# A second column of each gather chunk fetched row by row, shared by two queues

## The chip, the cores and the metric

The kernel runs on one core of one Trainium2 chip. The metric is the device time of one execution in microseconds (us). Before the change it is 22680.64 us, the median of three runs (22672.05, 22680.64, 22682.27).

## What is computed

Five graph layers run one after the other over the same graph of 12500 nodes (64 features each) and 412500 directed edges, sorted by destination. Four of them gather, for every edge, one row of a table by the edge's source node, weigh it, and sum over the edges of each destination:

```python
# RGAT, run twice (8 relations, 4 heads)
alpha = leaky_relu(qn[etype, dst] + kn[etype, src])
ex = exp(alpha - segment_max(alpha, dst)[dst]); attn = ex / segment_sum(ex, dst)[dst]
agg = segment_sum(attn[:, :, None] * xw[etype, src], dst)
# GAT, one head, no relations: the same with h[src]
# RGCN: segment_sum(xw[etypes, src] * norm, dst)
# GINE: segment_sum over src of relu(x[dst] + edge_feats), then a small two-layer network
```

Each layer's output is added to `x` after a layer norm and a relu at its input. The change touches the gathers of the first four layers.

## The kernel before

**Tiling.** The edges are padded to 128 partitions with 3224 edges each. A partition's edges are cut into 52 chunks (`CH`) of 62 columns (`J`), so a chunk is 128 x 62 edges. The layers are called CONV1, CONV2 (the two RGAT convolutions), GAT, RGCN and GINE. For each of the first four, a table is written to DRAM with one row per node, or per node and relation: 68 numbers (272 bytes) in CONV1 and CONV2, 65 (260 bytes) in GAT, 64 (256 bytes) in RGCN.

**A layer's chunk loop.** The loop body holds two chunks, b = 0 and b = 1, with their own half of the buffer `G` (part of the tile `region`), and runs 26 times.

- GpSimd (line 652, called from the loop at lines 764 to 773) waits on `idx_ready` for the chunk's indices and issues one indirect DMA per column, for columns 0 to 60 (`JP = J - 1` = 61 of them). Each brings 128 rows, one for each partition.
- SyncE (lines 605 to 619) fetches the last column, number 61, by 128 transfers of one row each. For each chunk it asks for a list of 128 row numbers from DRAM (607), waits for `idx_ready` (609) and for the list (611), and then eight times (`RUN` = 16) loads 16 row numbers into registers (613), copies them (614) and issues 16 row transfers (615). The source address is computed from the row number, times the length of a row, ahead of each transfer.
- In CONV1 alone, SyncE also issues one transfer per chunk (619) that writes zeros to a 2 MB stretch of `h_edge`, a table that GINE uses later.
- VectorE waits for all of the chunk's rows (semaphores `gathered` and `rows_in`), computes scores, weights and running sums, and releases the half of `G` by writing the indices of the chunk after next into `idx` (1911, in RGCN 1858), which raises `idx_ready`.
- ScalarE, in the layers with scores, copies last chunk's sums (870, 872) and sends them to DRAM (879), turns the query rows (896), asks for the next (899), spreads a mask (900), and then waits for VectorE's scores before it takes exponentials (905 to 908; 903 in GAT). In RGCN it copies matrices between the two steps of a ranking that TensorE and VectorE do in 16 quads of columns for the next chunk (944), and turns the four pieces of the sums (933, 936).

The order on each queue is the order of the code. A chunk can be consumed when both GpSimd's 61 columns and SyncE's 128 rows have landed. GpSimd and SyncE can each be up to two chunks ahead of VectorE, and no more.

The rows of all four layers' loops:

```python
for p0 in range(0, P, RUN):
    sp.load(indices, row_list[0:1, b, p0:p0 + RUN])
    for k, row in enumerate([sp.snap(r) for r in indices]):
        sp.dma_start(G[p0 + k:p0 + k + 1, b, J, :],
                     tables[l][bass.ds(row, 1), :]).then_inc(rows_in[l][b][2 * p0 // P], 16)
```

Of the kernel before, what the change touches and what calls it, by code (L numbers as in the profile page):

```python
# [9 lines left out]
BF16 = mybir.dt.bfloat16  # L10
ACT = mybir.ActivationFunctionType
# [53 lines left out]
JP = J - 1  # L65
RUN = 16
# [48 lines left out]
def build(nc, a, out):  # L115
    ctx = ExitStack()
    with ctx:
# [25 lines left out]
        row_lists = dram("row_lists", (2 * CH, P), I32)  # L143
# [23 lines left out]
        row_list = sb("row_list", [CH, 2, P], I32)  # L167
# [157 lines left out]
        act_s = sem("act_steps")  # L325
# [8 lines left out]
        rows_in = {l: [[sem(f"rows_in{l}_{b}_{k}") for k in range(2)] for b in range(2)] for l in SUMMED}  # L334
# [168 lines left out]

        block = ctx.enter_context(nc.Block())
# [3 lines left out]
        def _(sp):  # L508
# [13 lines left out]
            sp.dma_start(row_list[:, 1, :], a["src"].rearrange("(p c j) -> c p j", p=P, c=CH)[:, :, J - 1]).then_inc(loaded, 16)  # L522
            sp.dma_start(row_list[:, 0, :],
                         a["edge_type_8"].rearrange("(p c j) -> c p j", p=P, c=CH)[:, :, J - 1]).then_inc(loaded, 16)
# [6 lines left out]
            sp.dma_start(row_lists[0:CH, :], row_list[:, 0, :]).then_inc(list_in, 16)  # L531
            sp.dma_start(row_lists[CH:2 * CH, :], row_list[:, 1, :]).then_inc(list_in, 16)
            for l in LAYERS:
# [66 lines left out]
                kind = 0 if REL_OF[l] > 1 else CH  # L600
                for q in range(GP):
                    sp.wait_ge(stored[q], 16 * TURNS * (l + 1))
                if l == CONV1:
                    sp.wait_ge(list_in, 32)
                with sp.Fori(0, CH // 2) as i:
                    for b in range(2):
                        sp.dma_start(row_list[0:1, b, :], row_lists[bass.ds(i * 2 + (kind + b), 1), :]).then_inc(list_in, 16)
                        sp.wait_ge(idx_ready, i * 2 + ((CH + 2) * l + b + 1))
                        sp.sem_inc(chunk_begun, 1)
                        sp.wait_ge(list_in, i * 32 + 16 * (CH * l + b + 3))  # L610
# [39 lines left out]
        def _(pool):  # L650
# [55 lines left out]
            for l in LAYERS:  # L706
# [12 lines left out]
                if l == GINE:  # L719

                    pool.wait_ge(big_zero, 16 * CH)
# [56 lines left out]
        def _(act):  # L778
            steps = Steps(act, act_s)
# [29 lines left out]
            for l in LAYERS:  # L809
# [66 lines left out]

                def send_sums(i, b, O):
                    act.wait_ge(sum_ready, i * 2 + (CH * l + b + 1))
                    act.dma_start(sum_rows[:, bass.ds(i * (2 * J) + b * J, J), :], O).then_inc(sum_out, 16)

                if h:
# [9 lines left out]
                    act.wait_ge(loop_ok, l + 1)  # L891
                    def score_chunk(i, b, more):
                        nth = CH * l + b + 1
                        at = i * (2 * J) + b * J
                        act.wait_ge(e_in, i * 32 + 16 * nth)
# [4 lines left out]
                        act.copy(REP[:, 0:k, 1:J1], bc(cont[:, bass.ds(at, J)], 1, k)).then_inc(q_in, 1)  # L900
                        act.wait_ge(ex_in, i * 2 + nth)
# [16 lines left out]
                if l == RGCN:  # L918
# [27 lines left out]
                    def finish_chunk(i, b, ranks):  # L946
                        for n in range(NQ):
# [5 lines left out]
                        send_sums(i, b, O)  # L953

                    for n in range(NQ):
                        copy_turned(0, 0, n)
# [305 lines left out]
        def _(dve):  # L1262
# [37 lines left out]
            for g in range(TURNS):  # L1300
# [28 lines left out]
            stt(out=row_list[:, 0, :], in0=row_list[:, 1, :], scalar=float(REL), in1=row_list[:, 0, :], op0=ALU.mult,  # L1329
                op1=ALU.add).then_inc(lists_ready, 1)  # L1330
# [336 lines left out]
            for l in LAYERS:  # L1667
# [52 lines left out]
                nth = l  # L1720
                if l == RGCN:
                    dve.sem_inc(ew_free, 1)
# [113 lines left out]
                def weighted_sums(i, b, at, ranks):  # L1836
# [8 lines left out]
                    def piece_step(m):  # L1845
                        q = m // 2
                        if m % 2 == 0:
                            if q == 0:
                                dve.wait_ge(gathered[l][b], i * (16 * JP) + 16 * JP)
                                for half in range(2):  # L1850
                                    dve.wait_ge(rows_in[l][b][half], i * (8 * P) + 8 * P)
# [41 lines left out]
                with s.loop(CH // 2, 2 * per) as i:  # L1893
                    for b in range(2):
# [18 lines left out]
                        if h:  # L1913
# [33 lines left out]
                            for half in range(2):  # L1947
                                dve.wait_ge(rows_in[l][b][half], i * (8 * P) + 8 * P)
# [94 lines left out]
```

## Time and profile before

| | us |
|---|---|
| median of three runs | 22680.64 |
| span of the profiled execution | 22678.7 |
| GpSimd (POOL) busy | 16413.3 |
| VectorE (DVE) busy | 10606.0 |
| ScalarE (ACT) busy | 5421.1 |
| TensorE (PE) busy | 5315.0 |

The profile gives the span of its execution and no separate total; the span is 1.9 us below the median of the runs. The gather loops of CONV1, CONV2, GAT and RGCN run on GpSimd from 447 to 4411 us, 4779 to 8739, 9048 to 13008 and 13248 to 17208 us. GINE and the end fill the rest. "SPq" and "ACTq" are the instruction queues of SyncE and ScalarE; an instruction that issues a DMA is listed there and is not counted as busy time. A line of the timeline with x128 is merged from 128 instructions, and its second number is the time from the start of the first to the end of the last.

### The profile page before, as it was taken

The numbers are of one execution on the slowest core, as the hardware profiler recorded it, in microseconds if no ns is written. First come the engines' busy times: TensorE is split into PE (matmuls) and PEld (weight loads), VectorE is DVE, ScalarE is ACT, GpSimd is POOL, SyncE is SP. The second block draws the span as 40 slices with busy tenths as digits, with TensorE's granted clock in tenths as the row PEclk, the third lists the DMA queues.
The fourth block names the chain that finished last, engine by engine and source line by source line (L and its number), as shares of the span: only waits on it lengthen the run. The fifth ranks groups of instructions, "written<-read, shape, count | busy, mean of one in ns | idle before, by whom it ended". The sixth has DMA issues, their size and how long they took to land.

```text
span 22678.7 us, 201879 instructions
## 1 busy us (share of the span) xinstructions
PE 5315.0 (23%) x30665; PEld 3876.7 (17%) x30665; DVE 10606.0 (47%) x9480; ACT 5421.1 (24%) x4707; POOL 16413.3 (72%) x17069
## 2 busy tenths in 40 slices
PE   2000000020000001222222266666662222222201
PEld 1000000010000001222222255555552000000001
DVE  2444444324444443556566668888884111111167
ACT  1222222222222222111111132222221211121175
POOL 7777777677777776777777767777776777777733
PEclk9999999999999999666666655555555666666655
DMA  6333333332222222222222232222222222222164
GB/s 203 95 98 101 95 98 98 88 97 76 70 75 70 72 73 46 54 54 58 54 57 55 52 87 56 52 56 52 56 52 61 84 76 76 76 80 80 66 235 162
DMA packets 782414, 1839.84 MB, mean 81 GB/s; under 512 B 380834, under 2 KB 415306, under 8 KB 720302
## 3 DMA queue, kind: packets, MB, share of 16 engines
q0 software_dynamic: 544128, 569.36, 13.8%
q10 hardware_dynamic: 88736, 721.35, 8.1%
q1 hardware_dynamic: 148622, 541.43, 6.7%
q14 instruction: 915, 7.50, 0.1%
q8 instruction: 13, 0.21, 0.0%
HBM read 1007.43 MB, written 929.12 MB: 85 GB/s over the span
## 4 chain that ended last, share of the span: by engine, by line
POOL 55%; issue 24%; SPq 12%; DMA 3%; DVE 2%; PE 2%; ACT 1%; POOLq 0%; DVEq 0%; ACTq 0%
POOL region L652 41%; POOL by_src L742 12%; SPq L615 9%; SPq L613 3%; DMA region<-by_src 2%; DMA row_list<-row_lists 1%; POOL q_rel L713 1%; SPq L614 1%; PE ps L1207 1%; DVE region L1567 1%; DVE region L1538 0%; PE ps L1168 0%; POOL h_edge L725 0%; PE ps L1209 0%; POOL q_one L713 0%
## 5 line engine op out<-in xcount | busy, mean ns | idle before, releaser
L652 POOL DMA_INDIRECT region<-table,idx x12688 | 11972.1, 944 | 3941.9 <-issue 3873.2
L742 POOL DMA_INDIRECT by_src<-region,idx x3224 | 3122.7, 969 | 1007.9 <-issue 1001.5
L1950 DVE TENSOR_TENSOR region<-ps,region 128x248 f32<-128x248 f32 (+1 forms) x156 | 74.4, 477 | 3958.0 <-DMA region<-table,idx 1967.5
L1216 PE MATMUL ps<-ident,region 128*68 128x128 f32 (+1 forms) x3 | 1.3, 444 | 8044.9 <-DVE region L2013 8044.9
L1767 DVE TENSOR_TENSOR region<-ps,region 128x2048 bf16<-128x2048 f32 x833 | 1845.8, 2216 | 18.2 <-DVE region L1761 8.0
L870 ACT COPY region<-region 128x4216 f32<-128x4216 f32 (+1 forms) x156 | 1182.2, 7579 | 2477.7 <-DVE region L1996 2477.7
L1112 PE MATMUL ps<-region 98*128 98x128 f32 x6448 | 1657.9, 438 | 323.3 <-DVEq L1833 192.8
L1533 DVE CAST region<-src 128x62 f32 (+1 forms) x52 | 11.7, 224 | 3463.8 <-DMA by_src<-region,idx 3463.6
L1207 PE MATMUL ps<-region,ident 128*128 128x512 f32 (+1 forms) x832 | 809.5, 1062 | 3141.2 <-DVE region L1538 3141.2
L1112 PEld LDWEIGHTS ps<-region 98*128 98x128 f32 x6448 | 1455.9, 330 | 410.7 <-DVEq L1833 269.7
L1905 DVE TENSOR_TENSOR_SCAN region<-region,ps 128x1008 f32<-128x1008 f32 x624 | 1382.9, 2244 | 10.7
L1216 PEld LDWEIGHTS ps<-ident,region 128*68 128x68 f32 (+1 forms) x3 | 0.4, 150 | 8045.6 <-DVE region L2013 8045.6
L1902 DVE TENSOR_TENSOR ps<-region,ps 128x1008 f32<-128x1008 f32 x624 | 1192.1, 1940 | 105.2 <-ACT ps L906 96.2
L1916 DVE TENSOR_TENSOR_SCAN region<-region,ps 128x2016 f32<-128x2016 f32 x104 | 452.8, 4354 | 1582.6 <-ACT region L900 1582.6
L905 ACT ACTIVATE region<-ps 128x248 f32<-128x248 f32 (+1 forms) x156 | 50.5, 324 | 4560.1 <-DVE ps L1964 4560.1
L944 ACT COPY region<-ps 98x512 f32<-98x512 f32 x832 | 476.3, 572 | 2703.7 <-PE ps L1095 2702.0
L1065 PE MATMUL ps<-later,ident_b 128*128 128x512 bf16 x832 | 376.6, 453 | 2884.7 <-DVE region L1809 2884.7
L980 ACT COPY ps<-region 128x1008 f32<-128x1008 f32 x208 | 381.8, 1852 | 2143.0 <-DVE region L1538 2143.0
L1105 PE MATMUL ps<-region 128*98 128x128 bf16 x3224 | 540.5, 320 | 1150.6 <-DVE region L1819 1150.5
L1207 PEld LDWEIGHTS ps<-region,ident 128*128 128x128 f32 x832 | 175.9, 219 | 3376.2 <-issue 3376.2
L903 ACT ACTIVATE region<-ps 128x4032 f32<-128x4032 f32 x52 | 183.6, 3532 | 2235.6 <-DVE ps L1964 2235.6
L1819 DVE TENSOR_TENSOR region<-region,ps 98x512 f32<-98x512 f32 x832 | 552.2, 664 | 185.9 <-PE ps L1112 185.9
(291 smaller groups left out, 16216.1 us busy)
## 6 DMA issues: line engine op xcount, KB each, us to landing
sums<-region ACTq DMA_DIRECT2D x104, 2232.0 KB
region<-table SPq DMA_DIRECT2D x13312, 0.3 KB
sums<-region ACTq DMA_DIRECT2D x104, 1984.0 KB, 11.1
region<-table,idx POOLq DMA_INDIRECT x12688
region<-table SPq DMA_DIRECT2D x6656, 0.3 KB
region<-table SPq DMA_DIRECT2D x6656, 0.2 KB
sums<-region ACTq DMA_DIRECT2D x52, 2046.0 KB
region<-by_src SPq DMA_DIRECT2D x52, 2015.0 KB, 9.6
```

Of the source, the lines that this page charges most:

```text
L613: sp.load(indices, row_list[0:1, b, p0:p0 + RUN])
L615: sp.dma_start(G[p0 + k:p0 + k + 1, b, J, :], tables[l][bass.ds(row, 1), :]).then_inc(rows_in[l][b][2 * p0 // P], 16)
L652: pool.indirect_dma_start(out=to, out_offset=None, in_=table, in_offset=bass.IndirectOffsetOnAxis(ap=index, axis=0)).then_inc(s, 16)
L742: pool.indirect_dma_start(out=by_src, out_offset=bass.IndirectOffsetOnAxis(ap=idx[:, b, j:j + 1], axis=0), in_=MSG[:, b, j, :], in_offset= ...
L870: last = act.copy(O[:, :, 0:D + h], OT[:, 0:D + h, 1:J1].rearrange("p f j -> p j f"))
L1105: pe.matmul(ps[0:HI, 1, (j % QUAD) * LO:(j % QUAD + 1) * LO], HOT[RGCN][:, m % 2, j % GROUP, 0, 0:HI], HOT[RGCN][:, m % 2, j % GROUP, 1, : ...
L1112: last = pe.matmul(ps[:, 6 + n % 2, c * LO:(c + 1) * LO], AT[0:HI, n % 2, c * LO:(c + 1) * LO], BASE[0:HI, c, :], start=True, stop=True)
L1207: pe.matmul(o, ident[:, :], XS[:, :, 1 + j0:1 + j1].rearrange("p f j -> p j f"), start=True, stop=False)
L1767: tt(HOT[l][:, m % 2, 0:n], it, bc(HALF[l][1][b][:, js[0]:js[0] + n, :], 3, LO), ALU.is_equal).then_inc(ab_ready, 1)
L1819: tt(flat[0:HI, 0:w], flat[0:HI, 0:w], ps[0:HI, 1, 0:w], ALU.add).then_inc(h_add, 1)
L1902: return tt(wg[q % 2].rearrange("p (f j) -> p f j", f=PF), rows, bc(weight[q], 1, PF), ALU.mult)
L1905: return dve.tensor_tensor_scan(OT[:, piece(q), :].rearrange("p f j -> p (f j)"), REP[:, piece(q), :].rearrange("p f j -> p (f j)"), wg[q ...
```

## The change

- GpSimd gathers 60 columns instead of 61 (`JP = J - 2`). The last two columns are 256 row transfers per chunk. SyncE issues the first 160, ScalarE the other 96.
- The lists hold byte offsets into the table instead of row numbers, multiplied out once by VectorE at the start (three lists, for row lengths of 272, 260 and 256 bytes). Source and destination are addressed as bytes.
- SyncE loads 32 offsets at a time: five loads per chunk instead of eight.
- ScalarE issues its 96 rows for the next chunk in one burst of three loads of 32 in CONV1, CONV2 and GAT, between the mask (900) and the exponentials. In RGCN it issues them in twelve portions of 8, behind the first twelve copies of line 944.
- The zeros of `h_edge` are written in quarters: one transfer of 0.5 MB per chunk in each of the four layers.
- The row semaphores are shared by the four layers, cleared between them, and split into five groups of rows.

```diff
-JP = J - 1
-RUN = 16
+ROWED = 2
+JP = J - ROWED
+RUN = 32
+ROWS = ROWED * P
+SP_ROWS = 160
+ROW_GROUPS = [(0, 64), (64, 128), (128, 160), (160, 224), (224, 256)]
...
+        def row_place(l, b, k):
+            p, j = divmod(k, ROWED)
+            return slots(l)[1][p:p + 1, b, 1 + JP + j, :].bitcast(U8)
+
+        def row_bytes(l, at):
+            n = 4 * row_in(l)
+            return tables[l].bitcast(U8).rearrange("n f -> (n f)")[bass.ds(at, n)].unsqueeze(0)
...
-                        for p0 in range(0, P, RUN):
-                            sp.load(indices, row_list[0:1, b, p0:p0 + RUN])
+                        for k0 in range(0, SP_ROWS, RUN):
+                            sp.load(indices, row_list[b:b + 1, k0:k0 + RUN])
                             for k, row in enumerate([sp.snap(r) for r in indices]):
-                                sp.dma_start(G[p0 + k:p0 + k + 1, b, J, :],
-                                             tables[l][bass.ds(row, 1), :]).then_inc(rows_in[l][b][2 * p0 // P], 16)
-                        if l == CONV1:
-                            he = h_edge.rearrange("(p j) k -> p (j k)", p=P)
-                            sp.dma_start(he[:, bass.ds(i * (2 * J * D) + b * J * D, J * D)], zeros_d).then_inc(big_zero, 16)
+                                sp.dma_start(row_place(l, b, k0 + k), row_bytes(l, row)).then_inc(rows_in[b][row_group(k0 + k)], 16)
+                        he = h_edge.rearrange("(p j) k -> p (j k)", p=P)
+                        w = J * D // QUARTERS
+                        sp.dma_start(he[:, bass.ds(i * (2 * J * D) + (b * J * D + l * w), w)], zeros_d[:, 0:w]).then_inc(big_zero, 16)
...
+                def fetch_rows(b, k0, n):
+                    act.load(act_indices[0:n], row_list[b:b + 1, k0:k0 + n])
+                    for k, row in enumerate([act.snap(r) for r in act_indices[0:n]]):
+                        act.dma_start(row_place(l, b, k0 + k), row_bytes(l, row)).then_inc(rows_in[b][row_group(k0 + k)], 16)
+
+                def fetch_all(i, b):
+                    rows_begin(i, b)
+                    for k0 in range(SP_ROWS, ROWS, RUN):
+                        fetch_rows(b, k0, RUN)
...
                         act.copy(REP[:, 0:k, 1:J1], bc(cont[:, bass.ds(at, J)], 1, k)).then_inc(q_in, 1)
+                        if more:
+                            fetch_all(i + b if b else i, 1 - b)
                         act.wait_ge(ex_in, i * 2 + nth)
...
                                 copy_turned(i + b if b else i, 1 - b, n)
+                                if n == 0:
+                                    rows_begin(i + b if b else i, 1 - b)
+                                if n < (ROWS - SP_ROWS) // 8:
+                                    fetch_rows(1 - b, SP_ROWS + 8 * n, 8)
```

## Rows read from the trace of the kernel before

**Rows 1.** The page's costliest group: busy, mean ns | idle before, and what ended it.
```profile
L652 POOL DMA_INDIRECT region<-table,idx x12688 | 11972.1, 944 | 3941.9 <-issue 3873.2
```
**Rows 2.** Timeline of GpSimd in CONV1: start us, duration us, what, idle before.
```profile
4019.20 0.94 POOL L652 DMA_INDIRECT region<-table,idx  x1 [0.30 <-issue]
4020.45 0.94 POOL L652 DMA_INDIRECT region<-table,idx  x1 [0.30 <-issue]
```
**Rows 3.** Timeline of SyncE's queue in CONV1.
```profile
4013.75 0.23 SPq L607 DMA_DIRECT2D row_list<-row_lists  x1
...
4084.97 0.61 SPq L615 DMA_DIRECT2D region<-table  x2
4085.76 0.58 SPq L619 DMA_DIRECT2D h_edge<-zeros_d  x1
4086.55 0.27 SPq L607 DMA_DIRECT2D row_list<-row_lists  x1
4095.40 66.04 SPq L615 DMA_DIRECT2D region<-table  x128
...
4323.33 0.23 SPq L607 DMA_DIRECT2D row_list<-row_lists  x1
```
**Rows 4.** Timeline of VectorE at the last chunk of CONV1.
```profile
4472.89 0.59 DVE L1950 TENSOR_TENSOR region<-ps,region 128x248 f32<-128x248 f32 x1 [28.69 <-DMA region<-table]
```
**Rows 5.** Timeline of SyncE's queue at the start of CONV2.
```profile
4777.69 0.36 SPq L598 DMA_DIRECT2D region<-q_rel  x1
...
4849.83 0.23 SPq L607 DMA_DIRECT2D row_list<-row_lists  x1
4852.91 68.51 SPq L615 DMA_DIRECT2D region<-table  x128
...
4995.61 0.23 SPq L607 DMA_DIRECT2D row_list<-row_lists  x1
```
**Rows 6.** The same in GAT (first two rows) and in RGCN.
```profile
9623.12 0.23 SPq L607 DMA_DIRECT2D row_list<-row_lists  x1
...
9764.93 0.23 SPq L607 DMA_DIRECT2D row_list<-row_lists  x1
...
13619.38 0.91 SPq L607 DMA_DIRECT2D row_list<-row_lists  x1
...
13765.89 0.23 SPq L607 DMA_DIRECT2D row_list<-row_lists  x1
```
**Rows 7.** SyncE's instructions by line, CONV2 (first row CONV1): ns min/median/max.
```profile
L615 SPq DMA_DIRECT2D region<-table x18: 212/213/258, 4095.4 to 4103.9; - x18
...
L615 SPq FUSED_REGOPS  x9: 37/37/37, 4856.0 to 4859.3; - x9
L615 SPq MOVE region<-table x9: 29/29/29, 4856.1 to 4859.4; - x9
L615 SPq DMA_DIRECT2D region<-table x9: 224/225/225, 4856.2 to 4859.4; - x9
...
L613 SPq TENSOR_LOAD <-row_list x416: 1137/1230/3952, 4782.6 to 8666.4; - x139
...
L614 SPq FUSED_REGOPS  x832: 161/178/191, 4783.7 to 8667.9; - x167
```
**Rows 8.** At ScalarE's send of the sums: its timeline, then SyncE's row transfers (ns).
```profile
2021.72 0.35 ACTq L879 DMA_DIRECT2D sums<-region  x1
...
2027.47 0.36 ACTq L899 DMA_DIRECT2D region<-q_rel  x1
...
L615 SPq DMA_DIRECT2D region<-table x4: 492/936/952, 2022.7 to 2025.6; - x4
```
**Rows 9.** Waits (us in total, times, longest): ScalarE in CONV2, ScalarE and VectorE in RGCN.
```profile
ACT region L905 <- DVE ps L1964: 2222.7, 51, 71.7
...
ACT region L944 <- PE ps L1095: 2702.0, 781, 12.1
...
DVE ps L1854 <- DMA region<-table,idx: 429.4, 50, 9.4
```

More of the change, by code:

```diff
@@ L333, in build @@
         list_in = sem("list_in")
-        rows_in = {l: [[sem(f"rows_in{l}_{b}_{k}") for k in range(2)] for b in range(2)] for l in SUMMED}
+        rows_in = [[sem(f"rows_in{b}_{k}") for k in range(len(ROW_GROUPS))] for b in range(2)]
+        act_list_in = sem("act_list_in")
         dst_ready = sem("dst_ready")
@@ L778, in _ @@
         def _(act):
-            steps = Steps(act, act_s)
+            act_indices = [act.alloc_register(f"act_row{k}") for k in range(RUN)]
             act.sem_inc(free_a, 2)
@@ L875, in _, with ask_rows, rows_begin @@
                 sum_rows = sums[l].rearrange("(p j) f -> p j f", p=P) if l in SUMMED else None
+                def ask_rows(i, b):
+                    act.dma_start(row_list[b:b + 1, SP_ROWS:ROWS],
+                                  row_lists[bass.ds(i * 2 + (CH * ROW_KIND[l] + b), 1), SP_ROWS:ROWS]).then_inc(act_list_in, 16)
+                def rows_begin(i, b):
+                    act.wait_ge(idx_ready, i * 2 + ((CH + 2) * l + b + 1))
+                    act.sem_inc(chunk_begun, 1)
+                    act.wait_ge(act_list_in, i * 32 + 16 * (CH * l + b + 1))
+                    act.sem_inc(chunk_begun, 1)
+                def fetch_rows(b, k0, n):
[6 more added lines that the diff above has]
+                        fetch_rows(b, k0, RUN)
+                if l in SUMMED:
+                    for q in range(GP):
+                        act.wait_ge(stored[q], 16 * TURNS * (l + 1))
+                    if l == CONV1:
+                        act.wait_ge(list_in, 48)
                 def send_sums(i, b, O):
@@ L900, in score_chunk @@
                         act.copy(REP[:, 0:k, 1:J1], bc(cont[:, bass.ds(at, J)], 1, k)).then_inc(q_in, 1)
+                        if more:
+                            fetch_all(i + b if b else i, 1 - b)
                         act.wait_ge(ex_in, i * 2 + nth)
@@ L953, in finish_chunk @@
                         send_sums(i, b, O)
+                    ask_rows(0, 0)
+                    fetch_all(0, 0)
                     for n in range(NQ):
@@ L1328, in _ @@
             dve.wait_ge(loaded, 16 * 7)
-            stt(out=row_list[:, 0, :], in0=row_list[:, 1, :], scalar=float(REL), in1=row_list[:, 0, :], op0=ALU.mult,
-                op1=ALU.add).then_inc(lists_ready, 1)
+            done(stt(out=list_type, in0=list_src, scalar=float(REL), in1=list_type, op0=ALU.mult, op1=ALU.add))
+            settle()
+            done(ts_(row_list[:, :], list_type, 4.0 * row_in(CONV1), None, ALU.mult))
+            done(ts_(list_src, list_src, 4.0 * row_in(GAT), None, ALU.mult))
+            settle()
+            ts_(list_type, list_type, 4.0 * row_in(RGCN), None, ALU.mult).then_inc(lists_ready, 1)
             done(dve.tensor_copy(rel[:, :], src8[:, 0:EPP]))
@@ L1720, in _ @@
                 nth = l
+                if l:
+                    for b in range(2):
+                        for part in range(len(ROW_GROUPS)):
+                            dve.sem_clear(rows_in[b][part])
                 if l == RGCN:
@@ L1849, in piece_step @@
                                 dve.wait_ge(gathered[l][b], i * (16 * JP) + 16 * JP)
-                                for half in range(2):
-                                    dve.wait_ge(rows_in[l][b][half], i * (8 * P) + 8 * P)
+                                for part, (lo, hi) in enumerate(ROW_GROUPS):
+                                    dve.wait_ge(rows_in[b][part], i * (16 * (hi - lo)) + 16 * (hi - lo))
                             elif not ranks:
@@ L1946, in _ @@
                             dve.wait_ge(gathered[l][b], i * (16 * JP) + 16 * JP)
-                            for half in range(2):
-                                dve.wait_ge(rows_in[l][b][half], i * (8 * P) + 8 * P)
+                            for part, (lo, hi) in enumerate(ROW_GROUPS):
+                                dve.wait_ge(rows_in[b][part], i * (16 * (hi - lo)) + 16 * (hi - lo))
                             done(tt(Qs, qv, G[:, b, 1:J1, D:ri].rearrange("p j h -> p h j"), ALU.add))
```

39 lines of the change are left out of this document (26 added, 13 removed).

## The prediction

> **What bounds the kernel now.** I read the page first. Its costliest group is GpSimd's gather at line 652: 12688 of them, busy 11972 us and idle 3942 us in the short pauses between them [rows 1]. The timeline then shows one gather every 1.248 us, 0.94 us of work and 0.30 us of pause [rows 2]. All but 69 us of that idle time is this pause, named "issue" [rows 1]. So a chunk of 61 columns takes GpSimd 61 x 1.248 = 76.2 us, and 52 chunks take 3960 us, which is the length of each of the four loops.
>
> SyncE comes next, because every chunk also waits for its 128 rows. Between two list requests that are four chunks apart in CONV1, 4013.75 and 4323.33, lie 309.6 us, so 77.4 us per chunk [rows 3]. That is more than GpSimd's 76.2. SyncE falls behind by about 1.2 us per chunk. VectorE starts CONV1's last chunk at 4472.9 us, after 28.7 us of idle time that a row transfer ended [rows 4], 62 us after GpSimd's last gather (4411 us). CONV1 is paced by SyncE, the other three loops by GpSimd. But SyncE is close behind there too. Where nothing holds it, it takes 145.8 / 2 = 72.9 us per chunk in CONV2 [rows 5], 141.8 / 2 = 70.9 in GAT and 146.5 / 2 = 73.3 in RGCN [rows 6].
>
> **What GpSimd gains.** One column less is 1.248 us per chunk. 60 columns take 74.9 us, and 52 chunks 3895 us, so 65 us less per loop, 260 us in all. This is the whole gain that the removed gathers can give in the loops that GpSimd paces. In CONV1 there is more to win: down from SyncE's 4473 us to GpSimd's 447 + 3895 = 4342, so 130 us. All four together are 325 us. That needs SyncE to stay under 74.9 us per chunk.
>
> **What SyncE's chunk costs after.** A row is now three instructions: 37 ns of register arithmetic, 29 ns of move and 225 ns of transfer request [rows 7]. In CONV1 the request is 213 ns, and two rows take 0.61 us from the first's start to the second's end [rows 3, 7], so they follow each other every 0.397 us, and each instruction carries a pause of (397 - 213 - 37 - 29) / 3 = 39 ns. In CONV2 a row is then 291 + 3 x 39 = 0.408 us. Eight loads of 16 numbers at 1.23 us are 8 x 1.27 = 10.2 us with the pause, 16 copies at 0.178 are 3.5 us with theirs [rows 7], and 128 rows 52.2 us. That leaves 7.0 us of the 72.9 for the list, its wait, the loop's return and stalls.
> - Rows: with byte offsets there is nothing to multiply, so the arithmetic goes and a row is 0.408 - 0.076 = 0.332 us. 160 of them are 53.1 us: +0.9 against now.
> - Copies: 160 instead of 128, +0.9 us.
> - Zeros: a request of 0.58 us [rows 3] and two small instructions, +0.75 us, now in every loop. In CONV1 a transfer of 2 MB stands ahead of the list, and from the list's request to the first row pass 8.9 us, where CONV2 takes 3.1 [rows 3, 5]. Over all chunks CONV1's 77.4 us hold 128 x 0.397 = 50.8 of rows, 13.7 of loads and copies, and 12.9 of the rest. Less CONV2's 7.0 and the request's 0.75 that is 5.2 us, which I put down to the 2 MB. A quarter of the bytes, a quarter of that: +1.3 us in the other loops, -3.9 us in CONV1.
> - Loads: five of 32 numbers instead of eight of 16. No row shows a load of 32. If the cost is all per load, five cost 5 x 1.27 = 6.4 us, which is -3.8. If it is all per number (1.23 / 16 = 77 ns), five cost 12.5 us with their pauses, which is +2.3. A gain beyond the first, or a cost above the second, has nothing in the trace for it. I take the second: the only load in the trace moves 16 numbers in 1.23 us, over five times a one-row transfer request (0.225), and a piece of work that long is likelier made of its sixteen parts than of a start.
>
> Sum per chunk: 0.9 + 0.9 + 0.75 + 1.3 + 2.3 = +6.15 us. SyncE then needs 79.1 us in CONV2, 77.1 in GAT and 79.4 in RGCN. In CONV1 rows are +0.6, copies +0.9, loads +2.3 and the zeros -3.9: 77.3 us, as now. All are above GpSimd's 74.9, so SyncE paces all four loops. With loads at the low end the four are 71.2, 73.0, 71.0 and 73.3, all below it. The switch in CONV2 lies at (74.9 - 66.6) / 5 = 1.66 us for a load of 32.
>
> The Trainium skill has two figures for this load, and they disagree. "DMA: Bandwidth & Descriptors", section "Latency and other measured facts", gives a register load a floor of about 600 ns. By that floor the second sixteen would cost 0.63 us, an estimate of 1.86 us per load and a kernel of about 22,505 us. "Runtime: NRT & Kernel Launch", section "Instruction fetch mechanics", says such loads cost their time for each register even in bulk (about 200 ns, from HBM). That is the shape I take, though the trace's 77 ns per number is far below its figure.
>
> **What ScalarE does.** The request for the query rows is 0.36 us on SyncE and 0.36 on ScalarE [rows 5, 8], so I price a row the same on both. A burst is 3 x (2.5 + 0.9) + 96 x 0.332 = 42 us with dear loads, 38 with cheap ones. It stands ahead of the exponentials, where ScalarE now idles 2222.7 / 51 = 43.6 us per chunk [rows 9]. It fits, and if it ran over by some us, VectorE would finish the chunk that much later, while GpSimd and SyncE have the other half of `G` to fill. The list request and the waits behind it are for things long done. I cost ScalarE's part at nothing in CONV1, CONV2 and GAT.
>
> In RGCN the twelve portions are 0.6 to 1.2 us of load, 0.2 of copies and 2.7 of rows: 3.5 to 4.1 us each. VectorE's own chain per chunk is 76.2 less its idle 429.4 / 50 = 8.6 us, so 67.6 us [rows 9]. ScalarE idles 2702 / 781 = 3.5 us ahead of each copy of line 944 [rows 9], and the copy then starts a step of TensorE. About three portions fall into VectorE's idle time. The other nine overrun their gaps, more so where the sums are turned as well. I put 4 to 10 us on the chain: 72 to 78 us. That is hidden under SyncE's 79.4 us, and would not be under GpSimd's 74.9.
>
> **Sum.** Loop by loop against GpSimd's 3960 us: CONV2 52 x 79.1 less 1 us behind the last row, +150. GAT 52 x 77.1 - 1, +47. RGCN 52 x 79.4 - 1, +168. CONV1 -5. Together +360 us on the span of 22678.7, 23,039 us. The runs' median is 1.9 us above the span. The forecast is 23,040 us.
>
> **Rivals.**
> 1. *A load of 32 costs what one of 16 does* (or up to 1.66 us). Then SyncE stays under GpSimd, and the kernel is faster. The price is 22680 - 325 = 22,355 us, and with RGCN held by VectorE's chain at 72 to 78 us up to 22,515. For it: fewer loads would be pointless otherwise, and no row excludes a fixed part. Against it: it needs nearly all of the 1.23 us to be fixed. It decides below a load of about 2.1 us, where the gain in CONV1 balances the losses of the others. The floor in the Trainium skill, above, falls on this side.
> 2. *SyncE's and ScalarE's rows hold each other up.* While ScalarE's send of the sums is being worked off, SyncE's requests take 0.936 us instead of 0.213 [rows 7, 8]. A row then takes 0.936 + 0.184 = 1.12 us instead of 0.397. From 2022.7 to ScalarE's next request at 2027.5, 4.8 us, SyncE so loses 4.8 x (1 - 0.397 / 1.12) = 3.1 us to a send that covers 128 partitions. One 128th of that for each of ScalarE's 96 rows is 2.3 us per chunk, and 208 chunks make +480 on the forecast: 23,520 us, or more if a single row costs more than its share. Against it: a row is one short piece, and between requests both queues spend a third of their time on other instructions. The Trainium skill's "DMA: Bandwidth & Descriptors", section "Issuing engines are not separate DMA queues", says that SP and ACT share the DMA engines and that issuing from several only saves issue time, so it allows the saving that this change is after.
> 3. *The byte offsets don't remove the arithmetic* (or put a copy in its place). Then 160 x 0.076 = 12 us more per chunk, about +2500: 25,500 us. The slice's offset is the register itself, so I see no reason for it.
>
> **Chances.** Forecast (SyncE paces at 76 to 81 us, 22,800 to 23,400 us): 0.53. Rival 1: 0.27. Between the two (load of 1.7 to 2.2 us, 22,450 to 22,800): 0.08, mostly on the faster side. Rival 2: 0.10. Rival 3: 0.02. A change within 0.2% (45 us) is about what a measurement can't tell from none. Faster 0.33, same 0.05, slower 0.62. The range reaches from the low end of rival 1 to just above the forecast's own: 22,340 to 23,500. The forecast's own range is 22,800 to 23,400.
>
> **What would show it.** In the profile after, line 613's successor should show loads of about 2.4 us, five per chunk; 1.2 to 1.6 is rival 1. The rows should show a move and a request and no arithmetic. Two list requests two chunks apart should be 158 us apart in CONV2. GpSimd should have waits of about 4 us per chunk for the indices, and VectorE should wait for a row transfer, not for a gather. Requests well over 0.225 us in the middle of ScalarE's burst would be rival 2. The prediction is most open to the one duration that the trace doesn't have: 1 us on each load moves the kernel by about 1000 us while SyncE paces it.

## The result, and the profile after

The changed kernel takes 23,126.7 us, the median of four runs (23,112.1 to 23,138.6), beside 22,676.7 for the kernel before on the same chip (22,672.1 to 22,682.3). The ratio is 1.0198, 95% interval 1.0185 to 1.0212: 2% slower. The forecast of 23,040 lies 0.4% off, and the range holds the time. But the queue that it named as the pacer is not the one that paces, as the trace and the experiments show.

The page after: span, busy times, the chain that ended last by engine, and three groups (L674 is the gather, L652 before).

```profile
span 23110.3 us, 235926 instructions
...
PE 5345.1 (23%) x30665; PEld 3876.4 (17%) x30665; DVE 10619.5 (46%) x9483; ACT 5415.5 (23%) x4707; POOL 16217.7 (70%) x16861
...
ACTq 29%; issue 22%; POOL 16%; DVE 13%; ACT 10%; PE 5%; DMA 4%; DVEq 0%; POOLq 0%; SPq 0%
...
L674 POOL DMA_INDIRECT region<-table,idx x12480 | 11779.6, 944 | 4545.7 <-issue 3764.9
...
L1973 DVE TENSOR_TENSOR ps<-region,ps 128x1008 f32<-128x1008 f32 x624 | 1191.8, 1940 | 3573.7 <-ACT ps L961 3564.7
...
L960 ACT ACTIVATE region<-ps 128x248 f32<-128x248 f32 (+1 forms) x156 | 50.5, 324 | 4279.8 <-issue 4249.8
```

GpSimd issues 208 gathers less, 208 x 1.248 = 260 us. Against [rows 1], its idle time other than "issue" rose from 69 us to 4545.7 - 3764.9 = 781. So 712 us of new waits eat a gain of 260. The difference, 452 us, is close to the 432 us by which the span grew. The chain of what ended last says who makes GpSimd wait: 29% of it is ScalarE's instruction queue, 0% is SyncE's. The third group shows the other end of it, beside its row in the page before:

```profile
L905 ACT ACTIVATE region<-ps 128x248 f32<-128x248 f32 (+1 forms) x156 | 50.5, 324 | 4560.1 <-DVE ps L1964 4560.1
```

ScalarE still idles 4280 us there, nearly as long as before, but the idle time now ends in "issue" where it ended in VectorE's scores: its queue is busy issuing its own 96 rows. And the second group shows VectorE waiting 3565 us in all for ScalarE's exponentials, where it waited 96.

Loop by loop, from one loop's first gather to the next one's (RGCN: to the end of the span):

| us | before | after | difference | forecast |
|---|---|---|---|---|
| CONV1 | 4332 | 4382 | +50 | -5 |
| CONV2 | 4270 | 4374 | +105 | +150 |
| GAT | 4200 | 4334 | +135 | +47 |
| RGCN and the rest | 9430 | 9574 | +144 | +168 |

Two chunks in CONV2, the first with the loop's return in it, the second without: ScalarE's timeline after (L892 copies the sums, L927 sends them, L900 asks for the list, L949 and L953 are the turned queries and the mask, L912 is the rows, L960 to L963 the exponentials).

```profile
5800.73 7.69 ACT L892 COPY region<-region 128x4216 f32<-128x4216 f32 x1 [13.86 <-DVE region L2067]
...
5809.11 0.39 ACTq L927 DMA_DIRECT2D sums<-region  x1
5817.08 0.25 ACTq L900 DMA_DIRECT2D row_list<-row_lists  x1
5817.44 3.52 ACT L949 COPY ps<-region 128x2016 f32<-128x2016 f32 x1 [8.50 <-issue]
...
5821.62 1.84 ACT L953 COPY region<-cont 128x1984 f32 x1 [0.66 <-ACT ps L949]
5824.89 38.55 ACTq L912 DMA_DIRECT2D region<-table  x96
5863.49 0.38 ACT L960 ACTIVATE region<-ps 128x248 f32<-128x248 f32 x1 [40.02 <-issue]
...
5864.27 3.52 ACT L963 ACTIVATE region<-ps 128x4032 f32<-128x4032 f32 x1
5881.66 7.70 ACT L892 COPY region<-region 128x4216 f32<-128x4216 f32 x1 [13.87 <-DVE region L2067]
...
5890.05 0.40 ACTq L927 DMA_DIRECT2D sums<-region  x1
5890.65 0.24 ACTq L900 DMA_DIRECT2D row_list<-row_lists  x1
...
5895.10 1.84 ACT L953 COPY region<-cont 128x1984 f32 x1 [0.64 <-ACT ps L949]
5901.04 38.40 ACTq L912 DMA_DIRECT2D region<-table  x96
```

Read it as a ring. From the first copy to the next chunk's first copy no step waits for a row, a gather or SyncE. First come the sums' copies and their send (8.8 us), then the loop's return and the request for the list (5809.5 to 5817.4, 7.9 us), then the turned queries up to the burst's first load (4.5 us; the mask ends beside it). Three loads and 96 rows take 41.6 us (5821.9 to 5863.5), the exponentials 4.3 us, and then come 13.9 us in which VectorE makes the sums that ScalarE copies next. That is 80.9 us. The next chunk has no loop return: its list is asked for 0.6 us behind the start of the send, not 8.0. But its list lands only 7.4 us after the request. Most of that passes beside the turned queries and the mask; the first row comes 5.9 us behind the mask's start instead of 3.3, so the list costs some 2.7 us. This chunk takes 76.0. GpSimd's CONV2 loop, 4034 us for 52 chunks, gives 77.6 on average. The waits in CONV2 after (us in total, times, longest) agree:

```profile
ACT region L960 <- issue: 2117.9, 51, 43.9
DVE ps L1973 <- ACT ps L961: 1296.1, 51, 29.6
...
POOL region L674 <- DVE idx L1982: 148.1, 39, 7.7
```

VectorE is through with its scores at 5839.8 and stands idle for 24.6 us until ScalarE's burst is over, 1296 us per loop. GpSimd's waits for the released half of `G` are what is left of that behind its own work.

The new instructions in the trace after: duration in ns, min/median/max. The rows are of CONV2, the last one of RGCN.

```profile
L636 SPq TENSOR_LOAD <-row_list x260: 2032/2127/6506, 4830.9 to 8844.8; - x130
L638 SPq MOVE region<-table x8320: 29/29/38, 4833.7 to 8858.1; - x199
L638 SPq DMA_DIRECT2D region<-table x8320: 224/225/1197, 4833.8 to 8858.2; - x199
L912 ACTq DMA_DIRECT2D region<-table x4992: 234/235/990, 4834.0 to 8848.7; - x200
L910 ACTq TENSOR_LOAD <-row_list x156: 2131/2239/2422, 4831.1 to 8835.3; - x156
L910 ACTq TENSOR_LOAD <-row_list x602: 709/722/780, 13658.0 to 17597.2; - x151
```

A row is a move and a request, with no arithmetic. A load of 8 takes 0.72 us (on ScalarE), of 16 1.23 (on SyncE, [rows 7]), of 32 2.13 on SyncE and 2.24 on ScalarE.

### The profile page after: what moved, and what is told of

It reads as the page before. It is cut to its first block, busy times and chain, and to the rows that moved or that the text cites. A ratio compares the mean times of both kernels' runs of the same rounds, so it can differ in the third digit from the quotient of the medians.

```text
span 23110.3 us, 235926 instructions
## 1 busy us (share of the span) xinstructions
PE 5345.1 (23%) x30665; PEld 3876.4 (17%) x30665; DVE 10619.5 (46%) x9483; ACT 5415.5 (23%) x4707; POOL 16217.7 (70%) x16861
## 3 DMA queue, kind: packets, MB, share of 16 engines
q14 instruction: 1442, 11.81, 0.2%
## 4 chain that ended last, share of the span: by engine, by line
ACTq 29%; issue 22%; POOL 16%; DVE 13%; ACT 10%; PE 5%; DMA 4%; DVEq 0%; POOLq 0%; SPq 0%
ACTq L912 22%; POOL by_src L764 12%; ACTq L910 5%; ACT region L892 5%; DVE region L1976 5%; DMA row_list<-row_lists 4%; DVE ps L1973 4%; PE ps L1175 2%; POOL region L674 2%; ACTq L911 1%; DVE region L1901 1%; ACT region L1063 1%; DVE region L1838 1%; ACT ps L949 1%; ACT ps L1071 1%
## 5 line engine op out<-in xcount | busy, mean ns | idle before, releaser
L674 POOL DMA_INDIRECT region<-table,idx x12480 | 11779.6, 944 | 4545.7 <-issue 3764.9
L892 ACT COPY region<-region 128x4216 f32<-128x4216 f32 (+1 forms) x156 | 1182.2, 7578 | 2349.3 <-DVE region L2067 2349.3
L999 ACT COPY region<-ps 98x512 f32<-98x512 f32 x832 | 475.8, 572 | 2542.5 <-PE ps L1158 1877.7
L960 ACT ACTIVATE region<-ps 128x248 f32<-128x248 f32 (+1 forms) x156 | 50.5, 324 | 4279.8 <-issue 4249.8
L674 POOL DMA_INDIRECT region<-sums,end_i x490 | 520.6, 1062 | 160.0 <-issue 147.8
```

The costliest lines, as they stand in the source:

```text
L674: pool.indirect_dma_start(out=to, out_offset=None, in_=table, in_offset=bass.IndirectOffsetOnAxis(ap=index, axis=0)).then_inc(s, 16)
L892: last = act.copy(O[:, :, 0:D + h], OT[:, 0:D + h, 1:J1].rearrange("p f j -> p j f"))
```

## The experiments

Every time below is of one profiled execution unless a median is named. The kernel before took 22,656 us in the job of the first four, 22,678 in that of the next four, and 22,719 (median of seven) in that of the last three. So a difference of less than some 65 us between jobs is not read. "Per chunk" is the mean distance of the chunks' first gathers on GpSimd's timeline. The full table stands at the end of this section.

**One queue's rows at a time.** In e1, e2 and e3 single rows are replaced by block transfers that bring fixed table rows instead of the listed ones: ScalarE's 96 by two, SyncE's 160 by three, or both. The lists are still asked for and awaited. The gathered rows of the last two columns are therefore not those of the reference.

```diff
+        def block_rows(eng, l, b, part):
+            lo, hi = ROW_GROUPS[part]
+            to = slots(l)[1][lo // ROWED:hi // ROWED, b, 1 + JP:1 + J, :]
+            eng.dma_start(to, tables[l][lo:hi, :].rearrange("(p j) f -> p j f", j=ROWED)).then_inc(rows_in[b][part], 16)
...
-                    for k0 in range(SP_ROWS, ROWS, RUN):
-                        fetch_rows(b, k0, RUN)
+                    for part in (3, 4):
+                        block_rows(act, l, b, part)
```

> The changed kernel, but ScalarE's 96 single rows of each chunk are replaced by two transfers of consecutive table rows (64 and 32 rows), so the values of these rows are not the ones the graph asks for. Everything else stays, SyncE's 160 rows too. Theory A (ScalarE's own order sets the pace: its burst of 42 us stands ahead of the exponentials that VectorE waits for): the kernel falls to SyncE's own pace, about 75.0, 76.8, 74.9 and 74.9 us per chunk in the four loops, 22,500 to 22,650 us. Theory S (SyncE's 160 rows set the pace, as forecast): no change, 23,080 to 23,150 us.

Measured: 22,429 us, 71 below theory A's range and far from theory S.

> The changed kernel, but SyncE's 160 single rows of each chunk are replaced by three transfers of consecutive table rows, so the values of these rows are not the ones the graph asks for. ScalarE's 96 rows stay. Theory A: nothing or little changes, 23,000 to 23,130 us. Theory S: GpSimd paces, 22,350 to 22,550 us.

Measured: 22,980 us, 20 below theory A's range, and 430 above theory S's.

> Both replacements together: no single rows at all, GpSimd gathers 60 columns. Both theories: GpSimd paces all four loops at 74.9 us per chunk, 22,330 to 22,380 us. This is what the removed column is worth when nothing comes in its place.

Measured: 22,372 us.

Without any single rows the kernel is at GpSimd's 74.93 us in all four loops. SyncE's rows alone add 57 us to that. ScalarE's alone add 608. Both together add 755 (against the changed kernel, timed in another job). So about four fifths of the cost come with ScalarE's rows alone, and some 90 us only when both queues issue rows. In e2's CONV2 ScalarE's ring is nearly what it was in the kernel after, though SyncE has next to nothing to do; ScalarE's idle time is 0.7 us per chunk shorter:

```profile
ACT region L964 <- issue: 2080.9, 51, 42.2
DVE ps L1977 <- ACT ps L965: 1302.7, 51, 27.9
```

And SyncE's own pace can be read where nothing else holds it. In CONV2 of e1 and of e4 (below), VectorE waits for rows, and SyncE waits for its list alone, never for VectorE. SyncE's only wait in e1's CONV2:

```profile
SPq L640 <- DMA row_list<-row_lists: 91.8, 52, 3.4
```

These are SyncE's 52 list requests, first and last start:

```profile
L635 SPq DMA_DIRECT2D row_list<-row_lists x52: 257/264/270, 4648.5 to 8509.6; - x52
```
```profile
L629 SPq DMA_DIRECT2D row_list<-row_lists x52: 257/264/270, 4704.8 to 8608.7; - x52
```

Over 51 chunks that is 75.7 us alone (e1) and 76.5 with ScalarE's rows beside it (e4). The forecast had 79.1.

**The loop's return.** The same runs price a part of ScalarE's ring that the timeline after shows as 8 us. Here is ScalarE at the loop's return in e1, whose body lacks ScalarE's rows:

```profile
5583.44 0.38 ACTq L933 DMA_DIRECT2D sums<-region  x1
5584.24 0.25 ACTq L906 DMA_DIRECT2D row_list<-row_lists  x1
```

From the send to the list's request pass 0.8 us at the return in e1, and 0.6 in the other chunk. In the kernel after and in e2 it is about 8 and 0.6. In the kernel before, the next copy starts 0.7 us behind the send at the return and 0.5 in the other chunk. So the return costs ScalarE some 7 us more, 3.6 us per chunk, as soon as its single rows are written out in the loop's body, whatever SyncE does. No run takes the return out by itself. The queue that the page calls "instruction" moved 1442 packets in the kernel after, 864 in e1, 621 in e2 and 43 in e3. That makes the fetching of the longer bodies' instructions a candidate, which is not shown.

**The burst cut in two.** e4 issues 64 of the 96 rows where the change has them, and the other 32 behind the exponentials, in the 13.9 us that ScalarE waits for the sums. RGCN is as in the change.

```diff
-                            fetch_all(i + b if b else i, 1 - b)
+                            fetch_all(i + b if b else i, 1 - b, ROWS - 32)
...
                                            ACT.Exp).then_inc(rep_in, 1)
+                        if more:
+                            fetch_rows(1 - b, ROWS - 32, 32)
                         store_sums(i, b, O)
```

> The changed kernel with ScalarE's burst cut in CONV1, CONV2 and GAT: 64 rows where the burst was, 32 rows behind the exponentials, where ScalarE waits 13.9 us for VectorE's sums. Same rows, same work. Theory A: ScalarE's cycle falls by 13 to 14 us per chunk in these three loops, below SyncE's, and the kernel falls by about 144 + 40 + 167 us to 22,740 to 22,820 us, RGCN unchanged. Theory S: unchanged within 30 us.

Measured: 22,752 us, in theory A's range. No work was taken out; 32 rows only stand in another place, and 375 us went. The timeline in CONV2 (a chunk with the loop's return, as above):

```profile
5820.85 25.38 ACTq L912 DMA_DIRECT2D region<-table  x64
5856.56 0.38 ACT L960 ACTIVATE region<-ps 128x248 f32<-128x248 f32 x1 [37.13 <-DVE ps L2037]
...
5859.44 10.95 ACTq L912 DMA_DIRECT2D region<-table  x32
5874.72 7.70 ACT L892 COPY region<-region 128x4216 f32<-128x4216 f32 x1 [13.86 <-DVE region L2069]
```

The second part ends at 5870.4, before the sums are there, and the wait for the sums is 13.86 us as before: 32 rows for nothing. ScalarE's idle time again ends with VectorE's scores. VectorE no longer waits for exponentials but for rows:

```profile
DVE region L2023 <- DMA region<-table: 1195.5, 49, 29.8
...
POOL region L674 <- DVE idx L1984: 24.9, 16, 3.7
```

This is the state that the forecast described. SyncE is the pacer once ScalarE is out of the way, at 76.1, 76.5 and 75.2 us per chunk. GpSimd's own timeline shows little of it, as SyncE needs most of a loop to fall behind by as much as GpSimd may be ahead. The rest of SyncE's lag falls behind GpSimd's last gather of each loop, so the table at the end of this section does not hold it: from CONV2's first gather to GAT's pass 4288 us in e4, 4208 in e3.

**RGCN's portions.** e4 left RGCN at 79.2 us. Its timeline in the kernel after (L999 is the copy between the ranking's steps, L988 and L991 the turned pieces):

```profile
15067.39 0.39 ACTq L927 DMA_DIRECT2D sums<-region  x1
15073.39 0.25 ACTq L900 DMA_DIRECT2D row_list<-row_lists  x1
15073.81 0.59 ACT L999 COPY region<-ps 98x512 f32<-98x512 f32 x1 [5.66 <-issue]
15077.22 2.71 ACTq L912 DMA_DIRECT2D region<-table  x8
...
15146.92 0.39 ACTq L927 DMA_DIRECT2D sums<-region  x1
15147.52 0.24 ACTq L900 DMA_DIRECT2D row_list<-row_lists  x1
15147.92 0.59 ACT L999 COPY region<-ps 98x512 f32<-98x512 f32 x1 [0.24 <-issue]
15155.12 2.75 ACTq L912 DMA_DIRECT2D region<-table  x8
```

A portion fits the steady 3.3 us between two copies. Three things don't. The loop's return takes 6.0 us (15067.39 to 15073.39), where 0.6 pass in the other chunk. In the chunk without a loop return the first row comes 7.2 us behind the copy (15147.92 to 15155.12), since the list was asked for right behind the send of 2 MB. And portions 4 and 8 stand ahead of a turned piece that was due. e5 (e4 with one more edit) keeps the twelve portions but skips copies 4, 8 and 12, each of which stands ahead of a turned piece:

```diff
-                                if n < (ROWS - SP_ROWS) // 8:
-                                    fetch_rows(1 - b, SP_ROWS + 8 * n, 8)
+                                if n in SPOTS:
+                                    fetch_rows(1 - b, SP_ROWS + 8 * SPOTS.index(n), 8)
```

with `SPOTS = [0, 1, 2, 3, 5, 6, 7, 9, 10, 11, 13, 14]`.

> The split burst, and in RGCN ScalarE's twelve portions of 8 rows stand behind the copies 0 to 3, 5 to 7, 9 to 11, 13 and 14, not behind 0 to 11: no portion stands ahead of the turning of a piece (copies 4 and 8), where VectorE waited 2.0 to 2.5 us for TensorE. Theory: 2 to 4 us per chunk less in RGCN, so 100 to 200 us less than the split burst alone (22751 us), which is 22,550 to 22,650 us. If the RGCN loop is held by SyncE, nothing changes.

Measured: 22,604 us, 148 below e4, as expected. RGCN went from 79.2 to 76.6 us per chunk, the others stayed.

**The lists asked for one chunk earlier.** e6 is e5 with both queues' list requests a chunk earlier (ScalarE's for the chunk after next, once the half of `row_list` is read), with a semaphore for each half.

```diff
                                            ACT.Exp).then_inc(rep_in, 1)
+                        if ahead:
+                            ask_rows(i + 1, b)
                         if more:
                             fetch_rows(1 - b, ROWS - 32, 32)
...
+                def sp_chunk(i, b, more):
+                    if more:
+                        sp_ask(i + b if b else i, 1 - b)
                     sp.wait_ge(idx_ready, i * 2 + ((CH + 2) * l + b + 1))
```

> The kernel with the split burst and the new places in RGCN, and each list of offsets is asked for one chunk earlier, on both queues, with a semaphore for each half of the list buffer. Before, ScalarE's request stood right behind its 2 MB of sums, and the list landed up to 7.4 us later while the queue waited. Theory: RGCN loses the 7 us that ScalarE waits at its first copy, SyncE loses some 2 us per chunk, and GpSimd paces all four loops at 74.9 us: 22,360 to 22,430 us. If the wait for the list lies beside other waits, it stays at the run before it in this series.

Measured: 22,395 us, as expected, and below both kernels. The waits for lists were the last thing that held SyncE over GpSimd: in CONV2 SyncE waits 3.1 us in all for its list, where it waited 92.9 in e4, and in the other three loops it is now ahead and waits for VectorE (17 to 74 us per loop). GpSimd's group and, in CONV2, what VectorE waits for at the end of its scores:

```profile
L686 POOL DMA_INDIRECT region<-table,idx x12480 | 11778.1, 944 | 3910.5 <-issue 3816.6
```
```profile
DVE region L2039 <- DMA region<-table,idx: 1215.0, 51, 27.3
```

The wait is as long as e4's, but a gather ends it now, not a row. GpSimd's idle time other than "issue" is 94 us in the whole kernel. Most of the 209 us between e5 and e6 is the lag behind GpSimd's last gather (CONV1 50 us, CONV2 77, by the distance between the loops' first gathers), which the us per chunk below do not show.

**One column.** e7 is the change without its second column: 61 gathered columns, 128 rows on SyncE, none on ScalarE, with the byte offsets, the loads of 32 and the quartered zeros.

```diff
-ROWED = 2
+ROWED = 1
...
-SP_ROWS = 160
-ROW_GROUPS = [(0, 64), (64, 128), (128, 160), (160, 224), (224, 256)]
+SP_ROWS = 128
+ROW_GROUPS = [(0, 64), (64, 128)]
```

> The changed kernel with one column by rows instead of two: GpSimd gathers 61 columns, SyncE issues 128 rows in four loads of 32 byte offsets, ScalarE none. What is left of the change is the byte offsets, the loads of 32 and the quartered zeros. Theory: a row costs SyncE 0.32 us instead of 0.40, it stays below GpSimd's 76.2 us in all loops, and CONV1 loses the 60 us by which SyncE lagged: 22,590 to 22,610 us on this chip (the kernel before: 22,656).

Measured: 22,617 us, 60 below the kernel before in its job (that one took 22,678, not the 22,656 that the expectation started from). All four loops run at GpSimd's 76.17 us, and CONV1's lag of 62 us behind GpSimd [rows 4] is gone. So the byte offsets, the longer loads and the quartered zeros are together worth 60 us by themselves; no run parts them.

**Another share.** e8 is e6 with 152 rows on SyncE and 104 on ScalarE (`SP_ROWS = 152`, a thirteenth portion in RGCN).

> As the run with the early lists, but SyncE takes 152 rows and ScalarE 104 (13 portions in RGCN). Theory: if SyncE is still at or above GpSimd's 74.9 us in a loop, this takes 3 us per chunk off it and gains up to 100 us; if GpSimd already paces all loops, no difference within 15 us.

Measured: 22,404 us, the same as e6 within what one run can tell. With the lists early, neither queue's number of rows is the limit, and the share no longer matters. SyncE, with 8 rows less, now waits for VectorE in all four loops (125 to 234 us per loop).

**The lists alone.** e9 is the changed kernel with e6's lists and nothing else. The burst is whole.

> The changed kernel with one difference: each queue asks for its row list one chunk earlier, so that the list is there when the queue comes to it. The burst of 96 rows stays whole and RGCN's portions stay where the change has them. Theory A (ScalarE's cycle of about 77.6 us paces three loops, and its waits for lists are part of it, some 1.3 to 4 us per chunk): each loop comes down by 0.7 to 3 us per chunk, not quite to GpSimd's 74.9; time about 22,640 us (22,550 to 22,750). Theory B (the list waits lie beside the wait for the sums, which only grows when they go): about 23,100 us, no change. Theory C (the burst alone is what is too long, whatever the lists): also about 23,100.

Measured: 22,743 us, at the upper edge of theory A's range, in a job whose kernel before is 0.2% above the others'. The loops came down by 1.4, 1.8, 1.5 and 2.9 us per chunk: theory A's size, and B and C fall. The chain is still ScalarE's queue (31%). In the chunk without a loop return the burst now follows the mask at once:

```profile
5881.00 1.84 ACT L964 COPY region<-cont 128x1984 f32 x1 [0.64 <-ACT ps L960]
5884.31 5.89 ACTq L924 DMA_DIRECT2D region<-table  x17
```

In RGCN the early lists alone take 2.9 us, e5's moved portions alone 2.6, both 3.7.

**What a load costs.** e10 is e4 with SyncE's five loads of 32 cut into ten of 16.

```diff
-                        for k0 in range(0, SP_ROWS, RUN):
-                            sp.load(indices, row_list[b:b + 1, k0:k0 + RUN])
+                        for k0 in range(0, SP_ROWS, 16):
+                            sp.load(indices[0:16], row_list[b:b + 1, k0:k0 + 16])
```

> The kernel with the divided burst (64 rows, then 32 behind the exponentials), in which SyncE loads 16 numbers of its list at a time where it loaded 32: ten loads of about 1.27 us per chunk in place of five of 2.13, which is 1.9 us per chunk more. If a load costs a small fixed part and a price for every number, and SyncE's sum of work is just over GpSimd's 74.9 us: CONV1 and CONV2 at 77 to 78 us per chunk, GAT at 76 to 77, time 22,950 to 23,050 us. If SyncE has room that hides it: 22,750 us. If loads of 16 took no less than loads of 32 each: over 23,500 us.

Measured: 23,037 us, against e4's 22,752. The loads and the list requests in CONV2:

```profile
L636 SPq TENSOR_LOAD <-row_list x497: 1137/1232/3847, 4798.9 to 8694.7; - x166
```
```profile
L629 SPq DMA_DIRECT2D row_list<-row_lists x52: 253/265/280, 4787.8 to 8796.7; - x52
```

SyncE's pace is (8796.7 - 4787.8) / 51 = 78.6 us, 2.1 above e4's 76.5, where five more loads at 1.27 less five times 0.9 make 1.9. The time is in the expected range. So SyncE has no room in this kernel, and five loads more per chunk cost it about 285 us.

**The best version, timed.** e11 is e6 again, beside the kernel before.

> The kernel of e6 again (160 and 96 single rows as in the change; burst divided into 64 and 32, RGCN's portions away from the turned pieces, lists asked for one chunk earlier), timed against the kernel before for an interval. By its first look: 22,380 to 22,410 us, ratio to before about 0.9875. A ratio above 0.99 would say that the first look was a lucky one.

Measured: 22,399 us, median of four (22,396 to 22,401), ratio 0.9859, interval 0.9842 to 0.9875. The expected 0.9875 is its upper end. It is 3.2% below the changed kernel.

GpSimd's us per chunk by loop (e11 is as e6), and the time (of before and after the medians; GpSimd's own work for 60 columns is 74.9, for 61 76.2):

| | CONV1 | CONV2 | GAT | RGCN | us |
|---|---|---|---|---|---|
| before | 76.3 | 76.2 | 76.2 | 76.2 | 22,677 |
| after | 77.8 | 77.6 | 78.2 | 79.2 | 23,127 |
| e1, ScalarE by blocks | 74.9 | 74.9 | 74.9 | 75.1 | 22,429 |
| e2, SyncE by blocks | 77.0 | 77.0 | 77.5 | 78.4 | 22,980 |
| e3, both by blocks | 74.9 | 74.9 | 74.9 | 74.9 | 22,372 |
| e4, burst cut | 75.0 | 75.4 | 75.0 | 79.2 | 22,752 |
| e5, and portions moved | 74.9 | 75.3 | 74.9 | 76.6 | 22,604 |
| e6, and early lists | 74.9 | 75.0 | 74.9 | 75.6 | 22,395 |
| e7, one column | 76.2 | 76.2 | 76.2 | 76.2 | 22,617 |
| e8, e6 with 152/104 | 74.9 | 74.9 | 74.9 | 75.6 | 22,404 |
| e9, early lists alone | 76.4 | 75.8 | 76.7 | 76.3 | 22,743 |
| e10, e4 with loads of 16 | 76.4 | 77.4 | 76.0 | 79.3 | 23,037 |

## Why the prediction was right, and where it was not

The sign and the size were right, the queue was not. Two errors of opposite sign met, and that the number came out is luck: SyncE was put 2 to 4 us per chunk too slow, and ScalarE's ring, 74.6 us by the prediction's own numbers, was 3 to 5 us longer.

- **GpSimd's gain: right.** 60 columns take 74.9 us (e3, e6), and the floor with no rows at all is 22,372 us, against 22,355 in rival 1's sum.
- **The step that failed: ScalarE's part "costed at nothing".** The burst was well priced (42 us forecast, 41.6 measured). It was compared with the wrong thing: with ScalarE's idle 43.6 us at a period of 76.2 [rows 9]. The rest of ScalarE's ring is 76.2 - 43.6 = 32.6 us, and 32.6 + 42 is 74.6, 0.3 us under the 74.9 that was wanted. On top came three things that had no price. The largest is the loop's return with the rows in its body, some 7 us in every second chunk, 3.6 per chunk. The request for the list is 0.3 us. Its landing was called "long done" and was not, since the request stands right behind the send of the sums: 2.7 us in every second chunk, 1.3 per chunk. In the two chunks shown that makes 33.1 (76.1 less an idle time of 43.0 in the middle of the loop before) + 40.1 of burst beyond the mask + 3.6 + 0.3 + 1.3 = 78.4 us, and they took (80.9 + 76.0) / 2 = 78.5; the loop's average was 77.6. By this sum the ring would be about 74.8 us without the dearer return, an estimate, so with it gone ScalarE would hardly have held GpSimd up. The second half of that step, that a few us over would only delay VectorE, holds for one chunk. Here each chunk's ring starts where the last one ended, so the excess adds up to the end of the loop. e4 shows it from the other side: 32 rows moved into a wait of the same ring cost nothing.
- **SyncE's pace: the mechanism right, the size too large.** It was put at 77.3, 79.1, 77.1 and 79.4 us. With ScalarE out of the way (e1) it is 74.9, 75.7, 74.8 and 75.3. The load is the term with the largest error that the runs take apart. A load of 32 takes 2.13 us, not 2.46, so five are 1.7 us less. Its three lengths fit about 0.25 us and 0.06 for every number, nearer the price per number that was taken than the price per load of rival 1. The other 0.6 to 2.4 us lie in terms that were not taken apart (the zeros' +1.3 in the three later loops, and stalls). The row, 0.332 us forecast, was right in its parts (29 + 225 ns and two pauses). The switch of 1.66 us in the prediction holds the pause of 0.04 with the load; for the load alone it is 1.62, which changes nothing. By e1, SyncE alone would have cost 57 us over the floor, and the kernel would have been about 22,430: faster than before.
- **RGCN: the number by chance.** "72 to 78 us, hidden under SyncE" was 79.2 and hidden under nothing. The list's landing (e9), the portions ahead of turned pieces (e5) and the loop's return of 6 us are the part that was missing.
- **CONV1: -5 forecast, +50 measured.** SyncE did get faster there, from 77.4 us to 74.9 (e1), with 32 rows more; how much of that the smaller zeros give, no run shows. ScalarE's 77.8 took its place.
- **Rival 1** (cheap load) fell: 2.13 us is just above its switch of 2.1. Its outcome of 22,355 to 22,515 is nevertheless where e1 and e6 are. What kept the kernel from it was ScalarE, not the load.
- **Rival 2** (the two queues' rows hold each other up) is there, but small. The median request stays at 225 ns, and SyncE's pace in CONV2 rises from 75.7 (e1) to 76.5 (e4) with ScalarE's rows beside it. That is 0.8 us where the rival had 2.3. ScalarE's ring pays as well: GpSimd's pace in CONV2 is 77.0 us in e2 and 77.6 with SyncE's rows beside it. The Trainium skill's "DMA: Bandwidth & Descriptors", section "Issuing engines are not separate DMA queues", has issue time as what a second issuer saves. This trace agrees as far as it goes: the second issuer did save SyncE its 96 rows, and spent them on an engine with 0.3 us to spare by the sum above.
- **Rival 3** fell: no arithmetic stands ahead of a row.
- **What was to show it.** Of the signs that the prediction named, the waits of GpSimd (3 to 5 us per chunk) came. The two that were its own did not: VectorE waits for ScalarE, not for a row, and SyncE's list requests two chunks apart in CONV2 are at 155 us, which is ScalarE's pace. Looking at who releases VectorE was enough to see that the right number had the wrong reason.

GAT's ring, 78.2 us, has the same cause, as its timeline after shows:

```profile
11056.02 7.35 ACT L892 COPY region<-region 128x4030 f32<-128x4030 f32 x1 [17.39 <-DVE region L2067]
...
11064.35 0.24 ACTq L900 DMA_DIRECT2D row_list<-row_lists  x1
...
11065.47 0.24 ACT L953 COPY region<-cont 128x62 f32 x1 [0.63 <-ACT ps L949]
11074.45 38.44 ACTq L912 DMA_DIRECT2D region<-table  x96
```

The queries and the mask are short there, so they no longer cover the list's landing: the first row comes 9.0 us behind the mask's start (CONV2: 5.9). And the wait for the sums is 17.4 us instead of 13.9.

What stays open: what makes the loop's return dear, and why RGCN keeps 0.6 us over GpSimd in e6, where the return still takes 6 us. GpSimd's small lag in CONV2 (75.4 in e4) is put down to SyncE by its pace alone.

## What to carry to other kernels

Work that is put into an engine's idle time has to be compared with the period that is wanted, not with the one that is there. Walk the engine's whole ring, with every wait, loop return and request in it, and add. When a loop's body grows by hundreds of instructions, don't carry its old return over: here it went from under 1 us to 6 to 8. When several queues are near the same period, price all of them to a tenth of a microsecond per chunk, or the one costed at nothing is the pacer. Put such work behind the engine's own output that others wait for, and ask for small lists a turn earlier than a large send on the same queue.

## What the runs showed of the hardware

- A load of register values from on-chip memory costs about 0.25 us and 0.06 us per number: 0.72 us for 8 (ScalarE), 1.23 for 16 (SyncE), 2.13 and 2.24 for 32 (SyncE and ScalarE).
- A request of a few hundred bytes that stands right behind a 2 MB send on the same queue lands 7 us later (5890.65, "DMA row_list<-row_lists", in the chain of the kernel after: 7.4 us; in GAT 7.1). Where the loop's return puts 6.7 us between the two, it lands in 2.8 (GAT, 11148.55). Asked for one chunk earlier it costs its 0.25 us of issue.
- A one-row request takes 0.225 us on SyncE and 0.235 on ScalarE. Some take up to 1.2 us. In the kernel before, SyncE's long ones (0.94 us) stood behind ScalarE's send of the sums [rows 8].
- The return of ScalarE's loop takes 6 to 8 us from the send's start to the next instruction when the body holds single rows written out, 192 in two chunks (CONV2: 8.0 us to the list's request, RGCN: 6.0). Without them it takes 0.5 to 1.3 us (the kernel before, e1, e3, e7), though the loop sends the same sums.
